# The experts' second layer as seven block products in place of eight

## The chip, the cores and the metric

The kernel runs on one core of a Trainium2 chip. The metric is the device time of one execution in microseconds, median of the runs shown. The kernel issues work to TensorE (PE for its matmuls, PEld for its weight loads), VectorE (DVE), ScalarE (ACT), GpSimd (POOL) and the DMA queues of SyncE (SP).

## The reference

One layer of a graph network over 6,250 tokens of width 256, in float32. A graph attention part and a mixing part are added to `x`; then every token passes through a mixture of experts. All tokens share one routing decision, so the same 2 of 8 experts serve all of them. Only this last part is touched:

```
xf = layernorm(x)                                        # 6250 x 256
h = gelu(einsum('nd,edf->enf', xf, W1) + b1)             # per expert 6250 x 512
y = einsum('enf,efd->end', h, W2) + b2                   # per expert 6250 x 256
out = x + layernorm(sum over 2 experts of w_e * y_e + xf) * gamma + beta
```

## The kernel before

The tokens are cut into 25 blocks (`NB`) of 250 (`BT`), each of two token tiles (`TB`) of 125 (`TP`); in an output row a token has its own partition, 125 in all. Up to about 465 us of the profile the kernel makes the graph part, the mixing part, the residual and the normalised rows, which stay in SBUF. Then the routing picks two experts, their weights are loaded (`load_expert`, SP and ACT queues), and VectorE multiplies the second layer's weights `w2s` by the routing weights `tw` in place (L1803) and makes the offset row `b2w` (L1804, L1806). From there on only the experts run.

TensorE goes by a pipeline written out in program order: `hidden(b)`, then `result(b-1)`, for b from 1 to 25 (in the last step `result` alone). `hidden(b)` (L1231) makes eight tiles of 128 hidden features (`NF` = 4 for each of two experts) by 250 tokens, each over two halves of the width, in PSUM banks 0 to 3. ScalarE turns each tile to `ge` with gelu and the bias (L951), double buffered over blocks. `result(b)` (L1244) makes, for each of the two token tiles, one PSUM tile of 125 tokens by 256 outputs as a sum of eight matmuls, four for each expert; `ge` is the stationary operand (125 columns), `w2s` the moving one (256 columns). Its banks are 4 to 7, two for a block, so that two blocks are in flight.

A float32 matmul stands in the profile as two passes, each with its own weight load: 400 matmuls of `result` are "x800".

VectorE finishes a tile of 125 tokens n = 0 to 49: `make_z` adds the PSUM tile to the row `za` (L1826), takes the moments (L1828, L1830); `make_row` prepares the next `za` (L1815, L1818); `make_y` centres and scales by gamma (L1837) and, with the inverse deviation from POOL, makes the output row (L1844). POOL makes that deviation in `z_scale` (L663, L665) and adds beta to the residual row in `x_and_offset` (L671), in this order by tile. SP stores a block's output when its second tile is done (L494; for the last block each tile alone, L497).

Every wait is a semaphore wait written out in the instruction stream of its engine, and each engine works in program order. `idle_work` (L977) is a filler, matmuls of `ones` by `ident`, 128 moving columns, which keep TensorE going in gaps of the middle part; it has no part in the result.

Of the kernel before, what the change touches and what calls it, by code (L numbers as in the profile page):

```python
# [11 lines left out]
ALU = mybir.AluOpType  # L12
# [10 lines left out]
TOP_K = 2  # L23
CAPACITY_FACTOR = 1.25
TP = 125
TB = 2
# [31 lines left out]
def gps_layer(nc, x, idx_dst, idx_src, w_gnn, attn_l, attn_r, w_qkv, bn_gamma, bn_beta, w_dw, w_pw,  # L58
# [43 lines left out]
    with ExitStack() as ctx:  # L102
# [102 lines left out]
        skr = take(NH * BT)  # L205
        sqr = take(NH * BT)
        US = 3
        u = take(US * TB * D).rearrange("p (a t d) -> p a t d", a=US, t=TB)
        nsb = take(BT)
        vk = take(NH * BT)  # L210
# [16 lines left out]
        take = cut((0, LW, L))  # L227
        za = take(2 * D).rearrange("p (a d) -> p a d", a=2)

        def zc(b, c0, n=1):  # L230
            return Z[:, b * ZW + c0 * BT:b * ZW + (c0 + n) * BT]
# [125 lines left out]

        f_done = stage("f_done", TOP_K * NF)
        gelu_done = stage("gelu_done", TOP_K * NF)
        y_done = stage("y_done", TB)  # L360

        z_row = stage("z_row", 2)
        z = stage("z", 3)
        z_rstd = stage("z_rstd", 2)
        z_gam = stage("z_gam", 1)
        x_bet = stage("x_bet", 1)
# [55 lines left out]
        def res_bank(b, t):  # L422

            if b < NB - 1:
                return ps[0:TP, 6, t * D:(t + 1) * D]
            return ps[0:TP, (R_K, R_Q)[t], 0:D]

        def uses(b, ring):

# [74 lines left out]
        def _(pool):  # L504
# [161 lines left out]

            def x_and_offset(n):

                pool.wait_ge(z_row.sem, z_row.count(n, 1))
                at_ = x_of(n // TB, n % TB)  # L670
                g.tensor_tensor(at_, at_, bet[0:TP, :], ALU.add).then_inc(x_bet.sem, 1)  # L671

            pool.wait_ge(ln_in, 32)
            x_and_offset(0)
            for n in range(TB * NB):
                z_scale(n)
                if n + 1 < TB * NB:
                    x_and_offset(n + 1)

        @block.scalar  # L680
        def _(act):
# [262 lines left out]
            def gelu(b):  # L944
                for f in range(TOP_K * NF):
                    if b == 0 and f % NF == 0:
                        act.wait_ge(b1_in[f // NF], 16)
                    act.wait_ge(f_done.sem, f_done.count(b, f + 1))
                    if f == 0 and b >= 2:
                        act.wait_ge(y_done.sem, y_done.count(b - 2))  # L950
# [6 lines left out]
        def _(pe):  # L957
# [275 lines left out]
                    last.then_inc(f_done.sem, 1)  # L1233

            def result(b):
                for t in range(TB):
                    if b == 0 and t == 0:
                        pe.wait_ge(w_dve, 5)
                    if b >= 2:
                        pe.wait_ge(z.sem, z.count(TB * (b - 2) + t, 1))  # L1240
                    for f in range(TOP_K * NF):
                        if t == 0:
                            pe.wait_ge(gelu_done.sem, gelu_done.count(b, f + 1))
                        last = mm(ps[0:TP, 4 + 2 * (b % 2) + t, 0:D], ge[:, b % 2, f, t * TP:(t + 1) * TP],  # L1244
                                  w2s[:, f // NF, f % NF, :], start=(f == 0), stop=(f == TOP_K * NF - 1))
                    last.then_inc(y_done.sem, 1)
# [4 lines left out]
            pipeline(1, NB + 1, [(0, lambda b: hidden(b) if b < NB else None), (0, lambda b: result(b - 1))])  # L1251

        @block.vector
        def _(dve):
# [545 lines left out]
            for i in range(TOP_K):  # L1800
                dve.wait_ge(w2_in[i], 32)
                wi = w2s[:, i].rearrange("p f d -> p (f d)")
                v_.tensor_scalar(wi, wi, tw[:, i:i + 1], None, ALU.mult).then_inc(w_dve, 1)  # L1803
            v_.tensor_scalar(b2w[0:TP], b2s[0:TP, 0], tw[0:TP, 0:1], None, ALU.mult).then_inc(w_dve, 1)  # L1804
# [5 lines left out]
            def make_row(n):  # L1810

                b, t = n // TB, n % TB
                if n >= 2:
                    dve.wait_ge(z.sem, z.count(n - 2, 1))
                v_.tensor_scalar(za[0:TP, n % 2], x_of(b, t), mv2[0:TP, b, t, 0:1], rstd2[0:TP, b, t:t + 1],  # L1815
                                 ALU.subtract, ALU.mult).then_inc(z_row.sem, 1)
                dve.wait_ge(z_row.sem, z_row.count(n, 1))
                v_.tensor_tensor(za[0:TP, n % 2], za[0:TP, n % 2], b2w[0:TP], ALU.add).then_inc(z_row.sem, 1)  # L1818

            def make_z(n):  # L1820
                b, t, a = n // TB, n % TB, n % 2
                dve.wait_ge(z_row.sem, z_row.count(n))
                dve.wait_ge(y_done.sem, y_done.count(b, t + 1))
                if n >= 2:
                    dve.wait_ge(z_gam.sem, z_gam.count(n - 2))
                v_.tensor_tensor(zz[0:TP, a], ps[0:TP, 4 + 2 * (b % 2) + t, 0:D], za[0:TP, a], ALU.add).then_inc(z.sem, 1)  # L1826
                wait_apart(dve, z, z.count(n, 1))
                v_.bn_stats(zst[0:TP, a], zz[0:TP, a]).then_inc(z.sem, 1)  # L1828
                wait_apart(dve, z, z.count(n, 2))
                v_.bn_aggr(zmv[0:TP, a], zst[0:TP, a]).then_inc(z.sem, 1)  # L1830

            def make_y(n):
                b, t, a = n // TB, n % TB, n % 2
# [3 lines left out]
                v_.scalar_tensor_tensor(out=zg[0:TP, a], in0=zz[0:TP, a], scalar=zmv[0:TP, a, 0:1], in1=gam[0:TP],  # L1837
                                        op0=ALU.subtract, op1=ALU.mult).then_inc(z_gam.sem, 1)
                if t == 0 and b >= 2:
# [4 lines left out]
                v_.scalar_tensor_tensor(out=yo[0:TP, b % 2, t], in0=zg[0:TP, a], scalar=zr[0:TP, a, 1], in1=x_of(b, t),  # L1844
                                        op0=ALU.mult, op1=ALU.add).then_inc(y_ready.sem, 1)
# [55 lines left out]
```

## Time and profile before

| | |
|---|---|
| time, median of 3 runs | 822.78 us (822.64, 822.78, 825.34) |
| span of the profiled execution | 820.6 us |
| median time less that span | 2.2 us |
| the experts' part | from 471.9 us to the end |
| mean granted TensorE clock | 0.984 |
| TensorE matmul / weight load busy | 95% / 78% |
| VectorE / ScalarE / GpSimd busy | 63% / 52% / 47% |

The profiled execution's own time is not reported beside its span; the span runs from the first to the last instruction, and what lies around it is taken as the 2.2 us between the span and the median. Busy time of TensorE is the time in which at least one matmul is in flight, and matmuls are pipelined, so the spacing of matmuls says more than the share. "x32" at a row of the timeline is the number of passes that were merged into it, its duration reaching from the first one's start to the last one's end. A few matmul records can be missing.

### The profile page before, as it was taken

To read this page: it belongs to the slowest core of one execution; us is meant where nothing else is said; L and a number is where in the kernel's file an instruction comes from. 1 tells how busy PE (TensorE), PEld (TensorE's weight loads), DVE (VectorE), ACT (ScalarE), POOL (GpSimd) and SP (SyncE) were. 2 spreads that over 40 slices of the span, in tenths; PEclk is the share of its full clock that TensorE was granted. 3 is DMA by queue.
4 is the path that set the end of the run, shared out by engine and by line. 5 is a ranking of instruction groups with operands and counts; after the bars stand their busy time and mean duration, and the time that the engine had idled before them with its cause. 6 is when DMAs were issued, how large, how long until landed. Compare 5 with 4: busy or idle time off the path is not lost. (4 is left out here: it accounts for less than half of the span.)

```text
span 820.6 us, 15099 instructions
## 1 busy us (share of the span) xinstructions
PE 780.2 (95%) x5056; PEld 642.5 (78%) x5056; DVE 519.0 (63%) x1475; ACT 426.2 (52%) x969; POOL 383.1 (47%) x601
## 2 busy tenths in 40 slices
PE   5899999999899999999489999999999999999996
PEld 4778888888566676666256888888888888888885
DVE  6863488797779888888988534343434343444445
ACT  2566336898999898888376143232323232323230
POOL 3430888777458888888457402222222222222222
PEclk9999999999999999999889899999999999999999
DMA  8855122222012121111101130000000000000000
GB/s 213 203 161 151 42 59 51 56 54 53 16 51 66 33 66 32 53 56 40 42 24 30 37 99 21 19 21 18 21 17 21 18 21 17 22 17 22 17 22 29
DMA packets 35420, 41.31 MB, mean 50 GB/s; under 512 B 11520, under 2 KB 20696, under 8 KB 35339
## 3 DMA queue, kind: packets, MB, share of 16 engines
q1 hardware_dynamic: 22355, 30.71, 13.0%
q0 software_dynamic: 8000, 6.82, 3.8%
q10 hardware_dynamic: 4984, 2.79, 1.4%
q8 instruction: 40, 0.66, 0.3%
q14 instruction: 41, 0.34, 0.1%
HBM read 25.59 MB, written 14.60 MB: 49 GB/s over the span
## 5 line engine op out<-in xcount | busy, mean ns | idle before, releaser
L951 ACT ACTIVATE Z<-ps,b1s 128x250 f32<-128x250 f32 x200 | 93.5, 469 | 233.1 <-PE ps L1231 233.1
L1244 PE MATMUL ps<-Z 128*125 128x256 f32 x800 | 176.6, 380 | 0.0
L1231 PE MATMUL ps<-Z 128*128 128x250 f32 x800 | 173.2, 374 | 0.0
L1244 PEld LDWEIGHTS ps<-Z 128*125 128x125 f32 x800 | 150.2, 188 | 22.2
L1231 PEld LDWEIGHTS ps<-Z 128*128 128x128 f32 x800 | 151.7, 190 | 17.4
L663 POOL TENSOR_SCALAR zr<-zmv 125x1 f32<-125x1 f32 x50 | 11.1, 221 | 249.0 <-issue 240.1
L1025 PE MATMUL ps<-Z,L 128*128 128x250 f32 x600 | 126.9, 374 | 0.0
L1025 PEld LDWEIGHTS ps<-Z,L 128*128 128x128 f32 x600 | 113.9, 190 | 12.9
L1826 DVE TENSOR_TENSOR Z<-ps,L 125x256 f32<-125x256 f32 x50 | 21.2, 425 | 161.0 <-PE ps L1244 161.0
L1145 PE MATMUL ps<-wr,Z 128*125 128x256 f32 x400 | 92.7, 385 | 0.0
L790 ACT ACTIVATE Z<-Z,bn_o,bn_s 128x250 f32<-128x250 f32 x150 | 81.2, 598 | 1.0 <-DVE bn_o L1535 1.0
L1145 PEld LDWEIGHTS ps<-wr,Z 128*125 128x125 f32 x400 | 73.1, 188 | 10.2 <-issue 0.4
L1035 PE MATMUL ps<-Z,pw 64*64 64x250 f32 x600 | 54.6, 386 | 17.0 <-issue 15.3
L1416 DVE BATCH_NORM_STATS2 L<-Z 128x6 f32<-128x250 f32 x140 | 49.2, 408 | 26.4 <-ACT Z L786 24.2
L532 POOL DMA_INDIRECT L<-xt_table,idst x36 | 44.5, 1236 | 38.7 <-issue 37.6
L786 ACT ACTIVATE Z<-ps 128x500 f32<-128x500 f32 x75 | 43.4, 579 | 30.9 <-PE ps L1025 25.1
L1035 PEld LDWEIGHTS ps<-Z,pw 64*64 64x64 f32 x600 | 25.9, 134 | 38.0 <-issue 25.4
L535 POOL DMA_INDIRECT asrc<-xt_table,isrc x40 | 48.7, 1217 | 12.2 <-issue 12.2
L1004 PE MATMUL ps<-L,Z 128*125 128x264 f32 x200 | 51.8, 405 | 0.0
L1123 PE MATMUL ps<-L,ones 128*32 128x250 f32 x600 | 47.4, 377 | 1.5 <-issue 0.8
L1844 DVE SCALAR_TENSOR_TENSOR Z<-Z,zr 125x256 f32<-125x256 f32 x50 | 41.1, 822 | 9.5 <-POOL zr L665 6.2
L671 POOL TENSOR_TENSOR Z<-Z 125x256 f32<-125x256 f32 x50 | 36.1, 722 | 20.8 <-DVE L L1815 20.8
(221 smaller groups left out, 1274.7 us busy)
## 6 DMA issues: line engine op xcount, KB each, us to landing
Z<-in_x SPq DMA_DIRECT2D x25, 250.0 KB
out<-Z SPq DMA_DIRECT2D x24, 250.0 KB
xt_table<-L SPq DMA_DIRECT2D x25, 231.0 KB
Z<-in_x SPq DMA_DIRECT2D x1, 2016.0 KB
g_table<-gt SPq DMA_DIRECT2D x25, 62.5 KB
gr<-g_table SPq DMA_DIRECT2D x25, 62.5 KB
Z<-in_x SPq DMA_DIRECT2D x1, 1344.0 KB
Z<-in_w SPq DMA_DIRECT2D x2, 512.0 KB, 3.4
```

The costliest lines, as they stand in the source:

```text
L532: g.indirect_dma_start(rows_at[:, t, :], None, xt_table, bass.IndirectOffsetOnAxis(ap=idst[0:TP, j:j + 1].bitcast(U32), axis=0)).then_inc( ...
L535: g.indirect_dma_start(left_at[:, t, :], None, xt_table, bass.IndirectOffsetOnAxis(ap=isrc[0:TP, j:j + 1].bitcast(U32), axis=0), element_o ...
L790: a_.activation(zc(b, c), zc(b, c), ACT.Relu, bias=bn_o[:, c:c + 1], scale=bn_s[:, c:c + 1]).then_inc(done.sem, 1)
L951: a_.activation(ge[:, b % 2, f, :], ps[:, f % 4, 0:BT], ACT.Gelu, bias=b1s[:, f // NF, f % NF:f % NF + 1]).then_inc(gelu_done.sem, 1)
L1004: last = mm(ps[0:TP, 2 + 2 * (b % 2) + t, 0:XT], h_raw(b, k)[:, t * TP:(t + 1) * TP], wg[:, k, :], start=(k == 0), stop=(k == KD - 1))
L1025: last = mm(ps[:, group_bank(n), h * BT:(h + 1) * BT], wq[:, k, c * 128:(c + 1) * 128], h_raw(b, k), start=(k == 0), stop=(k == KD - 1))
L1035: return mm(to[cols_], lhsT[rows_, HALF * a:HALF * a + HALF], rhs[rows_], start=True, stop=True)
L1123: last = mm(ps[32 * q:32 * q + 32, 5, 0:BT], ones[:, 0:32], of, start=(i == 0), stop=(i == 3), skip_group_check=True)
L1145: last = mm(res_bank(b, t), ob(b, c, 1)[:, t * TP:(t + 1) * TP], wr[:, c, :], start=(c == 0), stop=(c == NO - 1))
L1231: last = mm(ps[:, f % 4, 0:BT], w1s[:, f // NF, k, (f % NF) * 128:(f % NF + 1) * 128], h_of(b, k), start=(k == 0), stop=(k == KD - 1))
L1244: last = mm(ps[0:TP, 4 + 2 * (b % 2) + t, 0:D], ge[:, b % 2, f, t * TP:(t + 1) * TP], w2s[:, f // NF, f % NF, :], start=(f == 0), stop=(f ...
L1416: v_.bn_stats(to, ps[:, group_bank(n), h * BT:(h + 1) * BT] if last else zc(b, c)).then_inc(z_sums.sem, 1)
```

## The change

For a block, write the hidden features of expert e and token tile t as A[e,t], and the weights of expert e and output half l (128 outputs) as W[e,l]. Before, each of four results Y[t,l] is the sum over the two experts of A[e,t] W[e,l]: eight block products, done as four pairs of width 256. After, they come from seven products (Strassen's scheme in the form with few sums), each of four matmuls (k = 0 to 3) with 125 stationary and 128 moving columns:

- POOL makes four sums of `ge` tiles for each block (`sums_of_g`, 125 x 500 of each, into `gs`, double buffered). It does so for block b+1 ahead of `z_scale` of block b.
- VectorE makes four sums of weight tiles once (`wt`, 128 x 512 each), between the scaling of `w2s` and the row `b2w`.
- TensorE issues the products in the order P1, P5, P6, P3, P7, P2, P4 into three banks (X, Z, Y = 4, 5, 6). P6, P7 and P4 accumulate onto bank X, P3 onto bank Z. Since each partial sum is read on the way, a product that reuses a bank waits for VectorE's read of it: P6 for that of P1, P3 for that of P5, P7 for that of P6, P4 for that of P7. One product lies between in each case. P1 of a block waits for all seven reads of the block before.
- VectorE reads each product with one `tensor_tensor` of 125 x 128 from PSUM (`take_parts`, seven for a block in place of two of 125 x 256), and the rest of a block's rows is regrouped: moments of both tiles, the next block's rows, centring, their offset, both outputs.
- The last block's `result` keeps the old form (`last_result`), with banks X and Y and a wait on all reads of the block before.

The diff, cut:

```diff
+            def sums_of_g(b):
+                a, n = b % 2, g_sums
+                pool.wait_ge(gelu_done.sem, gelu_done.count(b))
+                if b >= 2:
+                    pool.wait_ge(y_part.sem, y_part.count(b - 2))
+                g.tensor_tensor(gs[:, a, 0], ge_part(b, 0, 1), ge_part(b, 1, 1), ALU.add).then_inc(n.sem, 1)
+                pool.wait_ge(n.sem, n.count(b, 1))
+                g.tensor_tensor(gs[:, a, 1], gs[:, a, 0], ge_part(b, 0, 0), ALU.subtract).then_inc(n.sem, 1)
+                pool.wait_ge(n.sem, n.count(b, 2))
+                g.tensor_tensor(gs[:, a, 3], ge_part(b, 1, 0), gs[:, a, 1], ALU.subtract).then_inc(n.sem, 1)
+                g.tensor_tensor(gs[:, a, 2], ge_part(b, 0, 0), ge_part(b, 0, 1), ALU.subtract).then_inc(n.sem, 1)
             pool.wait_ge(ln_in, 32)
-            x_and_offset(0)
-            for n in range(TB * NB):
-                z_scale(n)
-                if n + 1 < TB * NB:
-                    x_and_offset(n + 1)
+            sums_of_g(0)
+            for t in range(TB):
+                x_and_offset(t)
+            for b in range(NB):
+                if b + 1 < NB - 1:
+                    sums_of_g(b + 1)
+                for t in range(TB):
+                    z_scale(TB * b + t)
+                if b + 1 < NB:
+                    for t in range(TB):
+                        x_and_offset(TB * (b + 1) + t)
...
+                for n in (P1, P5, P6, P3, P7, P2, P4):
+                    if n == P1:
+                        if b == 0:
+                            pe.wait_ge(w_dve, 3)
+                        else:
+                            pe.wait_ge(y_sum.sem, y_sum.count(b - 1))
+                        pe.wait_ge(gelu_done.sem, gelu_done.count(b))
+                    if n == P5:
+                        if b == 0:
+                            pe.wait_ge(w_sums, 4)
+                        pe.wait_ge(g_sums.sem, g_sums.count(b))
+                    if n == P6:
+                        pe.wait_ge(y_sum.sem, y_sum.count(b, KEPT_1))
+                    if n == P3:
+                        pe.wait_ge(y_sum.sem, y_sum.count(b, KEPT_5))
+                    if n == P7:
+                        pe.wait_ge(y_sum.sem, y_sum.count(b, KEPT_U))
+                    if n == P4:
+                        pe.wait_ge(y_sum.sem, y_sum.count(b, SUM_22))
+                    for k in range(NF):
+                        last = mm(ps[0:TP, bank[n], 0:HD2], of[n][:, k], by[n][:, k], start=(n in first and k == 0),
+                                  stop=(k == NF - 1), skip_group_check=True)
+                    last.then_inc(y_part.sem, 1)
+            def last_result(b):
+                for t in range(TB):
+                    if t == 0:
+                        pe.wait_ge(y_sum.sem, y_sum.count(b - 1))
...
+            v_.tensor_tensor(wt(1), half(0, 1), half(0, 0), ALU.subtract).then_inc(w_sums, 1)
+            v_.tensor_tensor(wt(3), half(1, 1), half(0, 1), ALU.subtract).then_inc(w_sums, 1)
+            dve.wait_ge(w_sums, 1)
+            v_.tensor_tensor(wt(2), half(1, 1), wt(1), ALU.subtract).then_inc(w_sums, 1)
+            dve.wait_ge(w_sums, 3)
+            v_.tensor_tensor(wt(4), half(1, 0), wt(2), ALU.subtract).then_inc(w_sums, 1)
...
+                for after, to, part, other, needs in (
+                        (P1, kz[0:TP, 0], x_, za[0:TP, 0, lo], None),
+                        (P5, kz[0:TP, 1], z_, za[0:TP, 1, hi], None),
+                        (P6, kz[0:TP, 2], x_, za[0:TP, 0, hi], None),
+                        (P3, zz[0:TP, 0, hi], z_, kz[0:TP, 2], KEPT_U),
+                        (P7, zz[0:TP, 1, hi], x_, kz[0:TP, 1], KEPT_5),
+                        (P2, zz[0:TP, 0, lo], y_, kz[0:TP, 0], KEPT_1),
+                        (P4, zz[0:TP, 1, lo], x_, za[0:TP, 1, lo], None)):
+                    dve.wait_ge(y_part.sem, y_part.count(b, after))
+                    if needs:
+                        dve.wait_ge(y_sum.sem, y_sum.count(b, needs))
+                    v_.tensor_tensor(to, part, other, ALU.add).then_inc(y_sum.sem, 1)
...
-            make_row(0)
-            for n in range(TB * NB):
-                make_z(n)
-                if n + 1 < TB * NB:
-                    make_row(n + 1)
-                make_y(n)
+            make_rows(0)
+            offset_rows(0)
+            for b in range(NB - 1):
+                take_parts(b)
+                dve.wait_ge(y_sum.sem, y_sum.count(b))
+                for t in range(TB):
+                    moments(b, t)
+                make_rows(b + 1)
+                for t in range(TB):
+                    center(TB * b + t)
+                offset_rows(b + 1)
+                for t in range(TB):
+                    make_y(TB * b + t)
```

## Rows read from the trace of the kernel before

**Rows 1.** The page: busy time and share of each engine.
```profile
PE 780.2 (95%) x5056; PEld 642.5 (78%) x5056; DVE 519.0 (63%) x1475; ACT 426.2 (52%) x969; POOL 383.1 (47%) x601
```

**Rows 2.** Busy time by stretch: us, then busy us (records) of each engine, clock, DMA.
```profile
600.00:700.00 100.00, 100.00 (x470) 88.34 (x470) 45.12 (x108) 26.98 (x58) 24.41 (x47) 1.00 0.06 19
```

**Rows 3.** The waits from 470 us on: engine, line, releaser, us, times, longest.
```profile
DVE Z L1826 <- PE ps L1244: 161.0, 24, 6.7
```

**Rows 4.** Timeline of one block: start us, us, engine, line, operation, merged count.
```profile
561.18 6.92 PE L1231 MATMUL ps<-Z 128*128 128x250 f32 x32
...
567.94 7.07 PE L1244 MATMUL ps<-Z 128*125 128x256 f32 x32
...
571.65 0.42 DVE L1826 TENSOR_TENSOR Z<-ps,L 125x256 f32<-125x256 f32 x1 [6.73 <-PE ps L1244]
...
574.85 2.49 PE L1231 MATMUL ps<-Z 128*128 128x250 f32 x11
```

**Rows 5.** Timeline: weight loads of fillers, and of matmuls with one moving column.
```profile
454.99 0.97 PEld L977 LDWEIGHTS ps<-ident,ones 128*128 128x128 f32 x8
...
461.83 0.97 PEld L1201 LDWEIGHTS ps<-ones,L 125*128 125x128 f32 x8
```

**Rows 6.** The filler's own line, all of its passes: ns minimum, median, maximum.
```profile
L977 PEld LDWEIGHTS ps<-ident,ones x118: 186/192/339, 16.2 to 471.7; 128*128 128x128 f32 x118
L977 PE MATMUL ps<-ident,ones x118: 275/276/582, 16.6 to 471.8; 128*128 128x128 f32 x118
```

**Rows 7.** Timeline: VectorE's end releases TensorE.
```profile
464.48 0.16 DVE L1751 TENSOR_TENSOR rtot<-rtot,ps 128x2 f32<-128x2 f32 x1 [1.05 <-PE ps L1201]
...
464.69 0.13 PEld L1206 LDWEIGHTS ps<-rt_w,rtot 128*1 128x1 f32 x4 [0.41 <-DVE rtot L1751]
```

**Rows 8.** Single lines, ns minimum, median, maximum: VectorE and POOL operations by inputs.
```profile
L1581 DVE TENSOR_TENSOR Z<-ps,L x25: 668/670/680, 213.5 to 442.9; 128x500 f32<-128x500 f32 x25
...
L1663 DVE SCALAR_TENSOR_TENSOR L<-ps,se,brow x50: 474/480/485, 227.7 to 455.2; 125x256 f32<-125x256 f32 x50
...
L1844 DVE SCALAR_TENSOR_TENSOR Z<-Z,zr x50: 485/877/883, 492.3 to 817.0; 125x256 f32<-125x256 f32 x50
```

**Rows 9.** Groups by form: a small POOL operation of the same kind.
```profile
L599 POOL TENSOR_TENSOR cc<-cc 125x2 f32<-125x2 f32 x25 | 4.8, 194 | 2.1
```

**Rows 10.** Timeline: POOL beside VectorE, twice in the experts' part, once before.
```profile
300.09 1.43 POOL L606 TENSOR_TENSOR Z<-Z,gr 125x256 f32<-125x256 f32 x2
...
300.95 0.88 DVE L1663 SCALAR_TENSOR_TENSOR L<-ps,se,brow 125x256 f32<-125x256 f32 x2
...
563.92 0.72 POOL L671 TENSOR_TENSOR Z<-Z 125x256 f32<-125x256 f32 x1
564.04 0.88 DVE L1844 SCALAR_TENSOR_TENSOR Z<-Z,zr 125x256 f32<-125x256 f32 x1
```

**Rows 11.** Timeline and landing: start of the experts' part.
```profile
475.89 0.42 SPq L490 DMA_DIRECT2D Z<-in_beta  x1
...
DMA to landing us min/median/max: 5.0/5.0/5.0
...
480.33 1.42 DVE L1803 TENSOR_SCALAR Z<-Z,tw 128x1024 f32<-128x1024 f32 x2 [0.92 <-DMA Z<-in_b]
...
485.94 7.07 PE L1244 MATMUL ps<-Z 128*125 128x256 f32 x32
```

**Rows 12.** Busy time by stretch around the last fall of the clock.
```profile
463.00:464.00 1.00, 0.81 (x7) 0.81 (x8) 0.40 (x3) 0.00 (x0) 0.00 (x0) 0.98 0.00 0
...
470.00:471.00 1.00, 1.00 (x7) 1.00 (x7) 0.00 (x0) 0.00 (x0) 0.00 (x0) 0.60 1.04 403
```

**Rows 13.** Timeline of the end.
```profile
800.29 13.98 PE L1244 MATMUL ps<-Z 128*125 128x256 f32 x64
...
814.36 0.42 DVE L1826 TENSOR_TENSOR Z<-ps,L 125x256 f32<-125x256 f32 x1
...
817.03 0.48 DVE L1844 SCALAR_TENSOR_TENSOR Z<-Z,zr 125x256 f32<-125x256 f32 x1 [0.82 <-POOL zr L665]
```

More of the change, by code:

```diff
@@ L207, in gps_layer @@
         US = 3
+        U0 = 2 * NC * BT + NC * BT + NO * BT + 2 * NH * BT
+        U1 = U0 + US * TB * D
         u = take(US * TB * D).rearrange("p (a t d) -> p a t d", a=US, t=TB)
@@ L226, in gps_layer @@
         yo = take(2 * TB * D).rearrange("p (a t d) -> p a t d", a=2, t=TB)
-        take = cut((0, LW, L))
-        za = take(2 * D).rearrange("p (a d) -> p a d", a=2)
+        take = cut((0, U0, L))
+        za = take(TB * D).rearrange("p (a d) -> p a d", a=TB)
+        gs = take(2 * 4 * NF * TP).rearrange("p (a i f n) -> p a i f n", a=2, i=4, f=NF)
+        kz = take(3 * 128).rearrange("p (i d) -> p i d", i=3)
+        take = cut((U1, LW, L))
+        wt0 = take(3 * NF * 128).rearrange("p (i f d) -> p i f d", i=3, f=NF)
+        take = cut((U0 - NF * 128, U0, L))
+        wt3 = take(NF * 128).rearrange("p (f d) -> p f d", f=NF)
         def zc(b, c0, n=1):
@@ L359, in gps_layer @@
         gelu_done = stage("gelu_done", TOP_K * NF)
-        y_done = stage("y_done", TB)
+        y_done = sem("y_done")
         z_row = stage("z_row", 2)
-        z = stage("z", 3)
+        z = stage("z", 2)
+        y_sum = stage("y_sum", 7)
+        y_part = stage("y_part", 7)
+        g_sums = stage("g_sums", 4)
+        w_sums = sem("w_sums")
         z_rstd = stage("z_rstd", 2)
@@ L426, in res_bank, with ge_part, wt @@
             return ps[0:TP, (R_K, R_Q)[t], 0:D]
+        X_BANK, Z_BANK, Y_BANK = 4, 5, 6
+        P1, P5, P6, P3, P7, P2, P4 = range(1, 8)
+        KEPT_1, KEPT_5, KEPT_U, SUM_12, SUM_22, SUM_11, SUM_21 = range(1, 8)
+        HD2 = D // 2
+        assert TB == 2 and TOP_K == 2 and HD2 == 128
+        def ge_part(b, e, t):
+            return ge[:, b % 2, NF * e:NF * e + NF, t * TP:(t + 1) * TP]
+        def wt(i):
+            return wt3 if i == 4 else wt0[:, i - 1]
         def uses(b, ring):
@@ L1250, in _ @@
             weights_of_two()
-            pipeline(1, NB + 1, [(0, lambda b: hidden(b) if b < NB else None), (0, lambda b: result(b - 1))])
+            pipeline(1, NB + 1, [(0, lambda b: hidden(b) if b < NB else None), (0, lambda b: result(b - 1) if b < NB else last_result(NB - 1))])
         @block.vector
@@ L1832, in make_y, with make_rows, offset_rows @@
-            def make_y(n):
-                b, t, a = n // TB, n % TB, n % 2
+            def make_rows(b):
+                if b:
+                    dve.wait_ge(y_sum.sem, y_sum.count(b - 1))
+                for t in range(TB):
+                    v_.tensor_scalar(za[0:TP, t], x_of(b, t), mv2[0:TP, b, t, 0:1], rstd2[0:TP, b, t:t + 1],
+                                     ALU.subtract, ALU.mult).then_inc(z_row.sem, 1)
+            def offset_rows(b):
+                for t in range(TB):
+                    dve.wait_ge(z_row.sem, 4 * b + 1 + t)
+                    v_.tensor_tensor(za[0:TP, t], za[0:TP, t], b2w[0:TP], ALU.add).then_inc(z_row.sem, 1)
@@ new lines, in _, with take_parts @@
+            lo, hi = slice(0, HD2), slice(HD2, D)
+            def take_parts(b):
+                dve.wait_ge(z_row.sem, 4 * b + 4)
+                x_, z_, y_ = (ps[0:TP, bank, 0:HD2] for bank in (X_BANK, Z_BANK, Y_BANK))
+                if b:
+                    dve.wait_ge(z_gam.sem, z_gam.count(TB * b - 1))
+                for after, to, part, other, needs in (
[10 more added lines that the diff above has]
+                    v_.tensor_tensor(to, part, other, ALU.add).then_inc(y_sum.sem, 1)
@@ L1834, in make_y, with moments, center @@
+            def moments(b, t):
+                n = TB * b + t
+                v_.bn_stats(zst[0:TP, t], zz[0:TP, t]).then_inc(z.sem, 1)
+                wait_apart(dve, z, z.count(n, 1))
+                v_.bn_aggr(zmv[0:TP, t], zst[0:TP, t]).then_inc(z.sem, 1)
+            def center(n):
+                t = n % TB
                 dve.wait_ge(z.sem, z.count(n))
```

57 lines of the change are left out of this document (29 added, 28 removed).

## The prediction

> **What bounds the kernel now.** I read the page first: TensorE is busy for 780 of 820.6 us and no other engine for more than 519 [rows 1]. An average says little about one stage, so I went to the busy time by stretch. The change touches only the part behind 471.9 us; between 600 and 700 us TensorE is busy for all of the 100 us, VectorE for 45, POOL for 24 [rows 2]. The waits agree: VectorE's longest total is 161 us spent on the result matmuls [rows 3]. The timeline then gives the unit. Hidden matmuls start at 561.18, results at 567.94, the next hidden ones at 574.85 [rows 4]: a block is 13.67 us, 6.76 for `hidden` and 6.91 for `result`, with no gap. 64 result passes in a row take 13.98 us [rows 13]; with 0.38 for the last, a pass starts every 13.60 / 63 = 0.216 us. So 32 x 0.216 = 6.91 us for a block's result, and whatever is saved there is saved in full as long as TensorE keeps its feed.
>
> **Removed and added on TensorE.** In 24 blocks 32 passes of 256 columns become 7 products x 4 matmuls x 2 passes = 56 passes of 128. By columns alone a pass would take 0.108 us (half of 0.216), 6.05 us for a block. But halving the columns leaves each weight load as large as before, and the load needs to fit in the shadow of the pass ahead. Passes of 128 columns with full loads stand in the trace as fillers: eight loads in 0.97 us at 0.192 each [rows 5, 6], so (0.97 - 0.19) / 7 = 0.111 us from one to the next. Loads for matmuls of one moving column come at the same spacing, (0.97 - 0.19) / 7 [rows 5]. So a load has a pace of about 0.11 us of its own and a pass of 128 columns the same: they just balance, side by side. I take 0.111: 56 x 0.111 = 6.22 us, 0.69 less than 6.91, and **24 x 0.69 = 16.6 us gained**. Bounds: 0.108 gives 20.6 us; 0.113, had a filler pass lost 2 ns more than its rows show by rounding, gives 13.9. Break even is at 6.91 / 56 = 0.123 us.
>
> The Trainium skill ("TensorE: Matmul & The Clock Gate", section "Back-to-back issue gap") speaks against the change: in a stream of load and matmul pairs of 128 columns it has about 81 ns a pair where the columns alone give 56, since both operations set the spacing. An estimate from that page's ratio, 1.45 x 0.108 = 0.156 us, would make a result 8.8 us and cost 45 us in all; the fillers at 0.111 don't agree with it.
>
> **The new loop between TensorE and VectorE.** Four products of a block wait until VectorE has read a product, and one product, 8 x 0.111 = 0.89 us, lies between. Let s be the start of a product's last pass. The pass ends at s + 0.28 [rows 6]. VectorE follows the modelled end by 0.09: the 16th result pass began at 567.94 + 15 x 0.216 = 571.18, ended 0.38 later, and VectorE began at 571.65 [rows 4]. Its read of 256 columns takes 0.42 and a like one of 500 takes 0.67 [rows 4, 8], about 1.0 ns a column, so one of 128 takes 0.29. TensorE answers 0.05 after VectorE's end (464.64 to 464.69) [rows 7]. Sum: s + 0.71. The waiting product's first load is wanted one pass ahead of its turn, at s + 0.89. Spare: about 0.18 us. I cost the four waits at nothing; the cover is the product between, and if it is gone each wait costs its lateness, 24 x 4 times.
>
> The seven reads must not be slowed by POOL, which makes its sums just then. Two SBUF inputs on VectorE do suffer: L1844 takes 0.485 alone and 0.877 in the median, and at 564.04 it ends 0.28 after POOL's L671 has ended [rows 8, 10], as if its 256 elements went only after POOL's operation. An operation with one input in PSUM doesn't: two of L1663 at 300.95 lie mostly inside POOL's 300.09 to 301.52 and all fifty take 474 to 485 ns [rows 8, 10]. The new reads are of this second kind.
>
> **VectorE between blocks.** Last read of a block to first of the next: 6.76 for `hidden` and 0.89 for P1. The work there is the old one regrouped: 45.12 us busy in 100 [rows 2] are 6.17 in a block of 13.67, less two reads of 0.42 [rows 4] 5.3, waits for POOL's beta additions included. With gaps of 0.1 between some six dependent ones it takes 5.9 us, and 7.3 are there. Hidden.
>
> **POOL.** L671 takes 0.72 for 256 elements [rows 10] and an operation of two takes 0.19 [rows 9], so 2.1 ns an element and 1.22 us for 500. Four sums with gaps of 0.1 take 5.2; what it did before is 24.41 us in 100 [rows 2], 3.3 a block; with locks that is under 10 of a block's 12.98 us. The sums of b+1 start when gelu of b+1 is done, beside result(b), and are wanted after hidden(b+2), 7 us after they end. z_scale stands behind them in POOL's order, but its moments come only after result(b). Hidden. ScalarE's new waits are on things done a block earlier; nothing.
>
> **The first block** is where the sums are late. Before, VectorE had w2 scaled at 481.75 and results began at 485.94 [rows 11]. Now POOL starts its four sums when beta has landed, 475.89 + 5.0 = 480.9 [rows 11]; VectorE's second scaling and its four weight sums (512 elements, 0.69 each by the 500's 0.67 [rows 8]) fall into them. If the lock goes operation by operation, each of POOL's runs about 1.1 after the other's end and each of VectorE's about 0.5: 4 x 1.15 + 5 x 0.5 + gaps = 7.4, so the weight sums are done at 488.4. Behind them stand six operations of 256 columns (two for b2w, two rows, two offsets), 0.4 each like L1826 [rows 4], and two waits of 0.6 for POOL's beta additions, since the offsets have two SBUF inputs: 3.6 in all, the first read at 492.0, its end at 492.3. P1 ends at 486.8, P5 runs 488.4 to 489.3, P6 and the other four from 492.4 to 496.9; without waits it would be 485.94 + 6.22 = 492.1. **Lost: 4.8 us.** Bounds: 0.3 if no lock shows, 5.5 if POOL's elements are slower than L671's.
>
> With TensorE idle for 1.6 and 3 us there, the clock may fall. Its last fall, from 2.4 to 1.2 GHz, came just before 464 us (0.98 in that us), when the stream had thinned, and it came back during 470 to 471 (0.60 is full speed in the last fifth), 6.8 us later [rows 12]. [...] Bounds 0 and 3.4 (half of those 6.8 us).
>
> **The last block.** Its result waits for all reads: with s as above for the last product of block 23, it starts at s + 0.71 and a load of 0.19 later. Its 16th pass starts at s + 0.9 + 15 x 0.216 = 4.1, and the first tile is ready 0.47 later, at 4.6. But VectorE has the 5.9 us of regrouped work behind its last read (s + 0.66 to 6.6) and takes it only at 6.6. A tile's chain from read to output is 817.51 - 814.36 = 3.15 us [rows 13], two one behind the other end at 12.9. In the old form the last pass starts at s + 32 x 0.216 = 6.9, and the end is 0.47 + 3.15 later, at 10.5. **Lost: 2.4 us.**
>
> **Sum** against the span: 820.6 - 16.6 + 4.8 + 2.2 + 2.4 = 813.4; with the 2.2 us between span and median, 815.6 us, 0.9% faster. What a measurement can tell from no change is 0.5%, 4.1 us.
>
> **The rivals.**
> - *The start is milder* (no clock fall, or little lock). For it: the clock fell only after thin work for a few us. It gives 804.8 (all low bounds) to 813.4. Chance 0.13; the forecast itself 0.55.
> - *The loop is late by a little.* If a read of 128 columns costs as much as one of 256 (0.42) and the answer takes 0.15, the sum is 0.94, late by 0.05; with slips at each product 0.06 x 4 x 24 = 5.8 us, 821.4: no change. For it: the spare is small. Against: durations follow the columns. 0.14.
> - *Slower: POOL's sums hold up the reads of PSUM.* A read then waits half a POOL operation, 0.56: the loop is 1.27, late by 0.39, 37 us in 24 blocks, 853. It decides from a lateness of 0.17 (4 x 0.17 = 0.69). Against: all fifty L1663. 0.09.
> - *Loads no longer hide*, since the fillers load the same `ones` each time and `ge` tiles differ: load and pass one after the other, 0.11 + 0.11 = 0.22 a pass, 12.3 for a result, 5.4 x 24 = 130 us, 953; anything above 0.123 is a loss. Against: the loads of L1201 differ too and keep 0.111 [rows 5]. 0.04. (The Trainium skill's section named above is a milder form of it.)
> - *POOL becomes the bound*, if its sums over strided tiles take 2.5 us instead of 1.22: 15.0 for a block against 12.98, 24 x 2.0 = 48 us, 864. Break even needs 2.1. Against: same operation and type as L671. 0.05.
>
> Faster by over 0.5%: 0.55 + 0.13 = 0.68. Within: 0.14. Slower: 0.09 + 0.04 + 0.05 = 0.18. The forecast's own terms reach from 806 to 820; taking in the little lateness, 806 to 823 holds 8 in 10.
>
> **What would show it.** In the changed profile: 56 result passes a block at 0.111 us (a block of 12.98), TensorE without idle at P6, P3, P7, P4; reads of 0.29 us; POOL's sums of 1.22 us ending before the block's reads do; VectorE's two-input operations near 482 to 491 us stretched, results of block 0 ending near 497, the clock perhaps at 0.5 there; an end some 5 us behind the last matmul. It would be wrong if a pass takes over 0.12, or if idle stands before each waiting product.

## The result, and the profile after

The changed kernel takes 810.03 us in the median of four runs (807.92 to 812.95) against 822.78 for the kernel before (822.64 to 825.34, four runs): ratio 0.984, 95% interval 0.981 to 0.987. The forecast was 815.6 with 806 to 823. The profiled execution is the fastest of the four; its span is 806.1 us, 14.5 less than before.

The page's first part and one stretch of the busy time by stretch answer to [rows 1, 2]. (Columns: engine, busy us, share, instructions; for the stretch: busy us of PE, PEld, DVE, ACT, POOL with records, granted clock, DMA share, GB/s.)

```profile
PE 762.1 (95%) x5632; PEld 643.2 (80%) x5632; DVE 549.7 (68%) x1599; ACT 426.4 (53%) x969; POOL 509.6 (63%) x697
```

```profile
600.00:700.00 100.00, 100.00 (x686) 94.52 (x685) 54.26 (x147) 29.54 (x63) 66.73 (x79) 1.00 0.07 22
```

TensorE is still without a gap, with more and shorter passes; POOL's work has nearly tripled and VectorE's has grown by a fifth, and neither shows in the time. One block in the timeline, to be set beside [rows 4] (start us, us, engine, line, operation, merged count, idle before and its releaser):

```profile
604.99 1.03 PE L1310 MATMUL ps<-Z 128*125 128x128 f32 x8
...
605.86 1.91 PE L1310 MATMUL ps<-L 128*125 128x128 f32 x16
606.16 0.29 DVE L1927 TENSOR_TENSOR L<-ps,L 125x128 f32<-125x128 f32 x1 [2.20 <-PE ps L1310]
...
607.07 1.15 POOL L708 TENSOR_TENSOR L<-L,Z 128x500 f32<-128x500 f32 x1
...
611.10 6.93 PE L1278 MATMUL ps<-Z 128*128 128x250 f32 x32
...
617.86 1.04 PE L1310 MATMUL ps<-Z 128*125 128x128 f32 x8
```

A block is 617.86 - 604.99 = 12.87 us (13.67 before), and its result 611.10 - 604.99 = 6.11 us (6.91 before). 6.11 / 56 is 0.1091 us a pass. From the first product of block 1 (501.96 us) to that of block 23 (785.25) every block takes 12.88 us, so 24 x (13.67 - 12.88) = 19.0 us are gained in the blocks with seven products. The single lines of the reads and of POOL's first sum (ns minimum, median, maximum):

```profile
L1927 DVE TENSOR_TENSOR Z<-ps,L x96: 291/292/293, 492.8 to 791.6; 125x128 f32<-125x128 f32 x96
L1927 DVE TENSOR_TENSOR L<-ps,L x72: 280/292/293, 490.4 to 788.1; 125x128 f32<-125x128 f32 x72
```

```profile
L706 POOL TENSOR_TENSOR L<-Z x24: 1246/1250/1277, 480.9 to 773.1; 128x500 f32<-128x500 f32 x24
```

No read of a product is longer than 0.293 us, though POOL's sums run beside them. What was given back lies at the two ends. The start, to be set beside [rows 11]:

```profile
480.37 2.41 DVE L1880 TENSOR_SCALAR Z<-Z,tw 128x1024 f32<-128x1024 f32 x2 [0.58 <-DMA Z<-in_b]
...
482.30 1.49 POOL L708 TENSOR_TENSOR L<-L,Z 128x500 f32<-128x500 f32 x1
482.81 1.53 DVE L1883 TENSOR_TENSOR L<-Z 128x512 f32<-128x512 f32 x1
...
486.31 1.03 PE L1310 MATMUL ps<-Z 128*125 128x128 f32 x8
...
488.18 1.14 PE L1310 MATMUL ps<-L 128*125 128x128 f32 x8 [0.83 <-DVE L L1888]
...
489.60 0.76 DVE L1906 TENSOR_TENSOR L<-L,Z 125x256 f32<-125x256 f32 x2
490.38 0.49 DVE L1927 TENSOR_TENSOR L<-ps,L 125x128 f32<-125x128 f32 x2
...
490.73 1.14 PE L1310 MATMUL ps<-L 128*125 128x128 f32 x8 [1.41 <-DVE L L1927]
...
495.20 6.93 PE L1278 MATMUL ps<-Z 128*128 128x250 f32 x32
```

VectorE's weight sum takes 1.53 us beside POOL's sum of 1.49, P5 starts at 488.18 and P6 at 490.73; block 0's result takes 495.20 - 486.31 = 8.89 us, 2.78 more than 6.11. The granted clock stays at 1.00 (2.4 GHz) in this execution. The end, to be set beside [rows 13]:

```profile
790.49 1.04 PE L1310 MATMUL ps<-L,Z 128*125 128x128 f32 x8
...
791.91 7.17 PE L1321 MATMUL ps<-Z 128*125 128x256 f32 x32 [0.39 <-DVE Z L1927]
...
797.03 0.41 DVE L1972 TENSOR_TENSOR Z<-ps,L 125x256 f32<-125x256 f32 x1
...
802.62 0.48 DVE L1950 SCALAR_TENSOR_TENSOR Z<-Z,zr 125x256 f32<-125x256 f32 x1 [0.82 <-POOL zr L691]
```

The last pass of block 23 starts at 790.49 + 7 x 0.109 = 791.25, and VectorE ends at 803.10, 11.85 later. In the profile before it is 10.5: block 23's last pass starts at 800.29 + 31 x 0.216 = 806.99, VectorE ends at 817.51 [rows 13]. That is 1.35 us lost. The first pass of all results comes 0.37 later than before (486.31 for 485.94 [rows 11]), from the part ahead, which the change does not touch. Together: -19.0 + 2.8 + 1.35 + 0.4 = -14.5, the whole difference of the spans.

### The profile page after: what moved, and what is told of

Its sections match the earlier page's. It is cut to its first block and busy times, and to the rows that moved or that the text cites. A ratio compares the mean times of both kernels' runs of the same rounds, so it can differ in the third digit from the quotient of the medians.

```text
span 806.1 us, 16493 instructions
## 1 busy us (share of the span) xinstructions
PE 762.1 (95%) x5632; PEld 643.2 (80%) x5632; DVE 549.7 (68%) x1599; ACT 426.4 (53%) x969; POOL 509.6 (63%) x697
## 5 line engine op out<-in xcount | busy, mean ns | idle before, releaser
L1278 PEld LDWEIGHTS ps<-Z 128*128 128x128 f32 x800 | 149.6, 189 | 17.4 <-DMA Z<-in_w 1.0
L1310 PE MATMUL ps<-L 128*125 128x128 f32 x576 | 71.1, 273 | 2.2 <-DVE L L1927 1.4
L1927 DVE TENSOR_TENSOR L<-ps,L 125x128 f32<-125x128 f32 x72 | 20.9, 292 | 75.4 <-PE ps L1310 75.4
L706 POOL TENSOR_TENSOR L<-Z 128x500 f32<-128x500 f32 x24 | 30.0, 1252 | 62.8 <-ACT Z L998 44.6
L1310 PEld LDWEIGHTS ps<-L 128*125 128x125 f32 x576 | 66.7, 188 | 2.6 <-DVE L L1927 1.6
L1927 DVE TENSOR_TENSOR Z<-ps,L 125x128 f32<-125x128 f32 x96 | 28.0, 292 | 55.8 <-PE ps L1310 55.8
L561 POOL DMA_INDIRECT asrc<-xt_table,isrc x40 | 48.4, 1210 | 12.2 <-issue 12.2
L698 POOL TENSOR_TENSOR Z<-Z 125x256 f32<-125x256 f32 x50 | 53.7, 1092 | 2.6 <-DVE L L1900 2.6
L689 POOL TENSOR_SCALAR zr<-zmv 125x1 f32<-125x1 f32 x50 | 13.1, 262 | 58.7 <-issue 47.7
```

Of the source, the lines that this page charges most:

```text
L561: g.indirect_dma_start(left_at[:, t, :], None, xt_table, bass.IndirectOffsetOnAxis(ap=isrc[0:TP, j:j + 1].bitcast(U32), axis=0), element_o ...
L1278: last = mm(ps[:, f % 4, 0:BT], w1s[:, f // NF, k, (f % NF) * 128:(f % NF + 1) * 128], h_of(b, k), start=(k == 0), stop=(k == KD - 1))
L1310: last = mm(ps[0:TP, bank[n], 0:HD2], of[n][:, k], by[n][:, k], start=(n in first and k == 0), stop=(k == NF - 1), skip_group_check=True)
L1927: v_.tensor_tensor(to, part, other, ALU.add).then_inc(y_sum.sem, 1)
```

## The experiments

Each median stands beside that of the kernel before, run together with it on the same chip. These medians of the kernel before differ by up to 1.4 us between sets (822.78 in the section above), so two versions are compared directly only where this column agrees, and otherwise by their distance from it.

| run | median us | before, same chip | ratio, interval |
|---|---|---|---|
| changed kernel again | 810.95 | 824.21 | 0.983 (0.981 to 0.985) |
| result in halves | 825.36 | 824.21 | 1.002 (1.000 to 1.003) |
| block 0 plain | 806.98 | 824.21 | 0.979 (0.977 to 0.981) |
| first and last block | 806.06 | 824.21 | 0.977 (0.975 to 0.980) |
| P4 uncovered | 828.33 | 823.49 | 1.006 (1.004 to 1.008) |
| late reads | 813.82 | 823.49 | 0.989 (0.985 to 0.993) |
| more sums (one run) | 816.24 | 823.49 | |
| bank 7 | 812.70 | 823.49 | 0.986 (0.983 to 0.989) |
| changed kernel, third | 810.47 | 823.07 | 0.984 (0.982 to 0.986) |
| fillers | 810.42 | 823.07 | 0.985 (0.983 to 0.988) |

**The changed kernel again.** No edit.

> The changed kernel once more, unaltered, with more runs, to see its spread. So far four runs gave 807.9, 808.2, 811.9 and 813.0 us. Theory A: the spread comes from the idle stretch of TensorE in the first block (487.3 to 490.7 us in the profile), after which the clock falls in some executions: the same two levels about 4 us apart should show, and the higher ones should have a lower mean clock. Rival B: the spread comes from the part ahead of the experts, where the clock falls once in every execution, and the first block has no part in it.

All five runs lie between 810.35 and 813.75 us. The profiled one, the slowest of them, shows what the first profile didn't: behind the idle stretch the clock is at half.

```profile
489.63 1.04 PE L1310 MATMUL ps<-Z 128*125 128x128 f32 x8
...
492.71 1.81 DVE L1906 TENSOR_TENSOR L<-L,Z 125x256 f32<-125x256 f32 x2
...
494.89 1.70 PE L1310 MATMUL ps<-L 128*125 128x128 f32 x8 [2.46 <-DVE L L1927]
...
501.03 5.24 PE L1278 MATMUL ps<-Z 128*128 128x250 f32 x24
```

```profile
494.00:495.00 1.00, 0.10 (x1) 0.11 (x2) 0.97 (x3) 0.00 (x0) 1.00 (x2) 1.00 0.00 0
...
496.00:497.00 1.00, 1.00 (x6) 1.00 (x6) 0.29 (x1) 0.00 (x0) 0.92 (x2) 0.50 0.00 0
...
499.00:500.00 1.00, 1.00 (x12) 1.00 (x11) 0.29 (x1) 0.00 (x0) 0.11 (x1) 1.00 0.00 0
```

From P6 to the next hidden layer 6.14 us go by (501.03 - 494.89) where the first profile has 4.47: 1.67 us of clock. And P6 itself comes 0.8 later, since the two offset rows took 1.81 us in place of 0.76: VectorE and POOL's beta addition took their turns in the other order. So the same program loses 2.8 or 5.3 us here. But the spread is not settled by it. Two levels 4 us apart didn't show in these five runs, and the slower ones have no lower mean clock (0.984 and 0.981 for the two slowest, 0.986, 0.984 and 0.982 for the others), so theory A failed. The kernel before spreads over 822.50 to 826.79 beside them, with no such idle stretch. The traces show a second place: the first product starts at 489.63 us here, at 486.31 in the first profile, though the program is the same. Of the 5.8 us between the two spans 3.3 arise ahead of the first product and 2.5 in block 0. That is rival B's place; why the part ahead varies was not looked into.

**Halving the columns alone.** The kernel before, with

```diff
-                    for f in range(TOP_K * NF):
+                    for l in range(2):
+                        cols = slice(l * 128, (l + 1) * 128)
+                        for f in range(TOP_K * NF):
...
-                        last = mm(ps[0:TP, 4 + 2 * (b % 2) + t, 0:D], ge[:, b % 2, f, t * TP:(t + 1) * TP],
-                                  w2s[:, f // NF, f % NF, :], start=(f == 0), stop=(f == TOP_K * NF - 1))
+                            last = mm(ps[0:TP, 4 + 2 * (b % 2) + t, cols], ge[:, b % 2, f, t * TP:(t + 1) * TP],
+                                      w2s[:, f // NF, f % NF, cols], start=(f == 0), stop=(f == TOP_K * NF - 1),
```

> The kernel before, with each result of 256 moving columns cut into two of 128, nothing else: 64 passes of 128 columns for 32 of 256 in each of 25 blocks, with twice the weight loads. Theory: loads of 125 columns hide behind passes of 128 and a pass costs 0.109 us as in the changed kernel's profile, 64 x 0.109 = 6.98 us for 6.91 in a block, 25 x 0.07 = 1.7 us slower in all. Rival: loads don't quite hide and the pace of the changed kernel has another cause: with 0.12 us a pass it is 19 us slower, with 0.156 some 77 us slower.

```profile
486.91 7.15 PE L1246 MATMUL ps<-Z 128*125 128x128 f32 x64
...
493.90 6.29 PE L1231 MATMUL ps<-Z 128*128 128x250 f32 x29
```

6.99 us for 64 passes, 0.109 each, and 1.2 us more in the median (2.0 by the traces' 0.08 a block; 1.7 expected). With twice the loads and unlike stationary tiles the load still hides. This settles the rival of loads that don't hide.

**Block 0 in the old form.** VectorE's four weight sums go behind the rows, and POOL's sums begin with block 1.

```diff
-            sums_of_g(0)
...
-(0, lambda b: result(b - 1) if b < NB else last_result(NB - 1))
+(0, lambda b: plain_result(b - 1) if b - 1 in (0, NB - 1) else result(b - 1))
```

> The changed kernel with block 0 in the old form (32 passes of 256 columns), so that VectorE makes the sums of the weights while TensorE works on block 0, and POOL makes no sums for it. Theory: block 0's result costs 6.91 us instead of the 8.89 from 486.31 to 495.20 us in the profile of the changed kernel, 2.0 us faster in span, 804.1 us; and since TensorE no longer stands idle there (theory A of the first run), no run lies 4 us above the others, so that the median gains 2 to 5 us. Rival B: the span gains 2.0 us and the spread stays.

```profile
484.75 0.68 DVE L1963 TENSOR_TENSOR L<-Z 128x512 f32<-128x512 f32 x1
...
486.32 7.07 PE L1334 MATMUL ps<-Z 128*125 128x256 f32 x32
...
493.23 6.92 PE L1292 MATMUL ps<-Z 128*128 128x250 f32 x32
```

With POOL's sums out of the way a weight sum takes 0.68 us, against 1.53 to 1.65. Block 0 takes 6.91 us, the span is 804.1 as expected, and the median falls by 4.0 us against the unaltered kernel run beside it. The spread (805.9 to 809.1) is as wide as before, so it has its source elsewhere. By these medians block 0's result takes 6.91 + 4.0 = 10.9 us in the changed kernel; against 6.11 it loses 4.8. Each of the two medians is known to some 1.7 us (from the intervals above), so the 4.8 is rough. The three profiles of the unaltered kernel have 8.9, 11.4 and 13.0 us, a loss of 2.8, 5.3 and 6.9.

**First and last block.** On top of it, the last block's first tile goes to bank 7, and VectorE interlocks its two tiles:

```diff
+                moments(b, t)
+                if t:
+                    make_y(TB * b)
+                center(TB * b + t)
+            make_y(TB * b + 1)
```

> As the run before, and the last block's first tile goes to the free bank 7, so that TensorE starts it without waiting for VectorE's last reads, while VectorE takes the second tile's sum before it finishes the first one's output. Theory: the last block loses 1.35 us in the changed kernel, since VectorE is still busy with block 23 and then handles two tiles one behind the other; with the tiles interlocked the end moves to 3.05 us behind TensorE's end, which itself is 0.6 us earlier: 1.0 to 1.5 us faster than the run before, a span of 802.8 us. Rival: VectorE's work of block 23 sets the start of the first tile and the gain is under 0.5 us.

```profile
789.26 1.04 PE L1321 MATMUL ps<-L,Z 128*125 128x128 f32 x8
...
790.14 7.07 PE L1334 MATMUL ps<-Z 128*125 128x256 f32 x32
...
797.43 0.42 DVE L1991 TENSOR_TENSOR Z<-ps,L 125x256 f32<-125x256 f32 x1
...
800.05 0.49 DVE L1955 SCALAR_TENSOR_TENSOR Z<-Z,zr 125x256 f32<-125x256 f32 x1 [0.52 <-DVE Z L1945]
```

From block 23's last product to VectorE's end 11.28 us go by where the changed kernel has 12.61: 1.3 us, as expected, and 0.9 in the median. The expected span of 802.8 us did not come in the profiled execution, which has 804.2: its first result pass starts at 487.07 for 486.32 in the run before, and 3.7 us follow VectorE's end where that run has 3.0. A gain of 0.9 between medians of five runs that spread over 3 us is not clear of noise; what shows the gain is the trace. This version has the lowest median, 806.06 us, 18 below the kernel before and 5 below the changed one.

**A wait without cover.** P4 directly behind P7.

```diff
-                for n in (P1, P5, P6, P3, P7, P2, P4):
+                for n in (P1, P5, P6, P3, P7, P4, P2):
```

> The changed kernel with P4 issued directly behind P7, whose read by VectorE it waits for, and P2 last: one of the four waits loses the product that covers it. It measures the loop from TensorE over VectorE and back. Theory: the loop from the start of a product's last pass to the next first load is 0.27 + 0.03 + 0.29 + 0.05 = 0.65 to 0.71 us, and without cover TensorE loses that, less 0.11 and plus a load that nothing hides (0.1 to 0.2): 0.65 to 0.8 us in each of 24 blocks, 16 to 19 us slower. Rival: the waits are satisfied otherwise than I read (the loop is longer, 1 us or more, hidden by the queue): over 24 us slower; or shorter, under 10.

```profile
607.71 0.29 DVE L1927 TENSOR_TENSOR Z<-ps,L 125x128 f32<-125x128 f32 x1 [0.58 <-PE ps L1310]
...
608.05 1.14 PE L1310 MATMUL ps<-L,Z 128*125 128x128 f32 x8 [0.38 <-DVE Z L1927]
...
609.90 6.93 PE L1278 MATMUL ps<-Z 128*128 128x250 f32 x32
...
623.42 3.76 PE L1278 MATMUL ps<-Z 128*128 128x250 f32 x17
```

A block is 13.52 us, 0.65 more. TensorE answers 0.05 us after the read's end (608.00). P7's last pass starts at 607.40, 0.31 ahead of the read, so the loop is 0.31 + 0.29 + 0.05 = 0.65 us; less the 0.11 until the next pass would have started and plus 0.10 for a load that nothing hides it is the 0.65 lost (rounded). The one cover taken away costs 24 x 0.65 = 15.6 us, more than the 13 us that the change gains in all. By the medians it is 17.4 to 18.1 us; what the other 2 are was not found, and the spread of such a set is as large.

**A longer loop.**

```diff
+                    v_.tensor_tensor(jz[0:TP, after - 1], part, za[0:TP, 0, lo], ALU.add).then_inc(jz_done, 1)
                     v_.tensor_tensor(to, part, other, ALU.add).then_inc(y_sum.sem, 1)
```

> The changed kernel with each of the seven reads of a product preceded by one more operation of the same form (125 x 128 from PSUM, into a tile that nobody uses), which makes the loop 0.29 us longer. The spare of the loop is read as 0.17 us. Theory: every one of the four waits becomes 0.12 us late, 0.5 us a block, 11 to 13 us slower in all, the break even with the kernel before. Rival: the spare is larger than 0.29 (VectorE's second read of a tile starts nearer to the end of the product): no change, within 2 us. If the spare were nil: 28 us slower.

```profile
609.69 1.98 PE L1312 MATMUL ps<-L 128*125 128x128 f32 x16
609.99 0.29 DVE L1929 TENSOR_TENSOR xg<-ps,L 125x128 f32<-125x128 f32 x1 [2.00 <-PE ps L1312]
610.20 0.28 DVE L1930 TENSOR_TENSOR L<-ps,L 125x128 f32<-125x128 f32 x1
```

The expectation of 11 to 13 us missed, and so did its rival of no change: a block is 12.95 us, only 0.07 more, all of it in the joined P5 and P6 (1.98 for 1.91). The miss is in what the edit added: of two operations with no wait between, the second starts 0.21 after the first, not 0.29. With that the sums fit: P1 is read from 0.41 behind its last pass's start, the others from 0.31. 0.41 + 0.21 + 0.28 + 0.05 = 0.95 is 0.07 to 0.08 past the 8 x 0.109 = 0.87 at which the next load is wanted, and 0.85 for the others is inside. The spare of the unaltered loop is 0.12 us at P6 and 0.22 at the other three. Against the kernel before the median is 2.9 to 3.6 us above the changed kernel's; the blocks account for 24 x 0.07 = 1.7 of it, the rest is within the spread of these four runs (812.25 to 817.64).

**Twice the sums on POOL.**

```diff
+                for i in range(4):
+                    if i >= 2:
+                        pool.wait_ge(jg_done, 4 * b + i - 1)
+                    g.tensor_tensor(jg[:, i % 2], ge_part(b, 0, 0), ge_part(b, 0, 1), ALU.subtract).then_inc(jg_done, 1)
```

> The changed kernel with four more sums of the same form on POOL in every block (from the same tiles, into tiles that nobody uses), ahead of the last real sum. Theory: POOL's work grows from 8.6 us in a block of 12.87 (66.7 us busy in 100) by 4 x 1.16 + gaps to 13.3 or 13.5 us, POOL becomes the bound and the kernel is 10 to 16 us slower, with VectorE's waits for POOL in the profile. VectorE's reads from PSUM keep their 0.292 us though POOL's sums now run beside all of them. Rival: POOL's sums hold up VectorE's reads as well: reads above 0.3 us and over 30 us slower.

POOL's groups between 600 and 700 us (line, operation, count, busy us, mean ns, idle before):

```profile
L716 POOL TENSOR_TENSOR xg<-Z 128x500 f32<-128x500 f32 x32 | 33.4, 1077 | 0.0
L700 POOL TENSOR_TENSOR Z<-Z 125x256 f32<-125x256 f32 x15 | 12.0, 818 | 0.0
L708 POOL TENSOR_TENSOR L<-Z 128x500 f32<-128x500 f32 x8 | 10.0, 1250 | 2.7 <-ACT Z L1004 2.7
```

The expectation was wrong: a block stays at 12.88 us. POOL is busy for 94.9 of these 100 us, 12.2 in a block, and just fits. I had taken 4 x 1.16 for the new sums, which take 4.2 together, and had added them to a busy time that held waits: the beta addition, 1.10 in the mean in the changed kernel, takes 0.82 here, twice a block. 8.6 + 4.2 - 0.6 = 12.2. This single run is 5.4 to 6.0 us slower against the kernel before than the changed kernel. Block 0 bears part of that: its P5 waits 6.0 us for POOL's last sum, and its result takes 503.53 - 487.92 = 15.6 us where the unaltered profiles have 8.9 to 13.0. The reads keep 0.29 us.

**Bank 7 alone.** The last block's first tile in bank 7, VectorE as it was.

```diff
-                    if t == 0:
+                    if t:
                         pe.wait_ge(y_sum.sem, y_sum.count(b - 1))
```

> The changed kernel with the last block's first tile in the free bank 7, so that TensorE needn't wait for the last reads of block 23; VectorE's order is unchanged. Theory: TensorE starts 0.6 us earlier, but VectorE is busy with block 23 until 797.1 us and takes the first tile no earlier, so the end doesn't move: within 0.2 us in span. Rival: TensorE's wait sets the end and it comes 0.6 us earlier.

```profile
796.93 1.04 PE L1310 MATMUL ps<-L,Z 128*125 128x128 f32 x8
...
797.80 7.07 PE L1321 MATMUL ps<-Z 128*125 128x256 f32 x32
...
809.05 0.48 DVE L1950 SCALAR_TENSOR_TENSOR Z<-Z,zr 125x256 f32<-125x256 f32 x1 [0.82 <-POOL zr L691]
```

TensorE starts 0.87 behind P4's start in place of 1.42, and VectorE ends 809.53 - 796.93 = 12.60 behind it, as before (12.61). The end is VectorE's. The spans can't show it: this one is 812.6 us, since its first product starts at 490.04 and its block 0 takes 11.6 us. The median, 10.8 us below the kernel before where the unaltered kernel is 12.6 to 13.3 below, shows no gain either.

**Idle time or clock.**

> The changed kernel unaltered, as the measure for the run beside it, on the same chip. In the profiled executions of it and of its relatives so far the first block's result took 8.9 us with the clock at full speed throughout (one of them), and 11.4 to 11.8 us where the clock fell to half behind the idle stretch (four). I expect the second.

```diff
                         if b == 0:
+                            idle_work(7, 3)
                             pe.wait_ge(w_sums, 4)
...
                     if n == P6:
+                        if b == 0:
+                            idle_work(7, 9)
                         pe.wait_ge(y_sum.sem, y_sum.count(b, KEPT_1))
```

> The changed kernel with twelve filler matmuls (128 x 128 by 128 columns, into the free bank 7) in the first block, three in front of the wait of P5 and nine in front of the wait of P6, in time that TensorE otherwise idles. They tell the idle time from the fall of the clock. Theory: of the 5.3 us that the first block loses when the clock falls, 1.6 us are work at half speed; with fillers the clock stays up, the block's result takes 9.0 to 9.8 us in the profile, and the median is 1.5 to 2 us below the unaltered kernel's. Rival: the fall of the clock costs nothing by itself, since TensorE waits for VectorE at that time anyway: the same median within 0.5 us, or above it where the fillers come late.

The control, then the fillers (PE records of both; for the control also the us in which the clock fell, the columns as in the busy time by stretch above):

```profile
493.01 2.07 PE L1310 MATMUL ps<-L 128*125 128x128 f32 x8 [2.46 <-DVE L L1927]
...
500.44 5.87 PE L1278 MATMUL ps<-Z 128*128 128x250 f32 x27
```

```profile
492.00:493.00 1.00, 0.00 (x0) 0.00 (x0) 0.97 (x3) 0.00 (x0) 1.00 (x2) 0.65 0.00 0
```

```profile
489.46 2.17 PE L1024 MATMUL ps<-ident,ones 128*128 128x128 f32 x18
...
492.10 1.14 PE L1313 MATMUL ps<-L 128*125 128x128 f32 x8 [0.47 <-DVE L L1930]
...
496.56 6.93 PE L1278 MATMUL ps<-Z 128*128 128x250 f32 x32
```

In the profiles it went by the theory: the control's clock is at half from 492.3 to 499.1 us and P6 to hidden takes 7.43 us, 2.96 more than the 4.47 at full clock; with fillers it takes 4.46 at full clock. The sizes were off: the control's result takes 13.0 us for the 11.4 to 11.8 expected, the filler run's 9.9. The medians, 810.47 and 810.42 us, don't differ, so the expected gain of 1.5 to 2 us did not come, and by the time alone it went by the rival. One execution each can't say whether the timed ones kept the clock; what the clock costs in the median stays open. The wait for VectorE is the same in both, P6 3.9 and 3.8 us late.

## Why the prediction was right, and where its sizes were off

The direction, the mechanism of the gain and the places of both losses held; the time came out 5.6 us below the point and inside the range. Three costed terms were off, all on the pessimistic side: the pass by 2.4 us, the first block by 2.2, the last by 1.05. A gain of 0.9% was forecast and 1.6% came. The time also lies within what the rival of a milder start gave (804.8 to 813.4), and the first profile, with no fall of the clock and 2.8 us lost, is that rival; the other two profiles of the same kernel, with the fall, are not.

- **The pass.** 0.111 us was taken, 0.1091 measured: 19.0 us gained for 16.6. The lower bound by columns alone (0.108) was nearer. The fillers load 128 stationary columns and the products 125, with 128 moving columns in both. In the filler run both stand in block 0 at full clock: 18 filler passes start 0.112 us apart, those of the products 0.109. The ratio is that of 128 to 125, which speaks for the load as what sets the fillers' spacing; products of 128 columns were not tried.
  The Trainium skill ("TensorE: Matmul & The Clock Gate", "Back-to-back issue gap") has both operations set the spacing at 128 columns. The size of its effect, 81 ns for 56, does not show in this float32 stream: halving the columns alone costs 0.08 us a block.
- **The loop.** Summed to 0.71 with a spare of 0.18; measured 0.65, and 0.75 at P6, with a spare of 0.22 and 0.12. At P6 it was tighter than forecast. Costed at nothing, rightly: no idle stands before P6, P3, P7 and P4 after block 0. That one product of cover is what holds it was shown by taking it away (0.65 us a block).
- **POOL beside the reads.** An operation with one PSUM input is not held up, 168 reads at 0.280 to 0.293 us; one with two SBUF inputs is, a weight sum takes 0.68 us without POOL's sums and 1.53 to 1.65 beside them. POOL's 1.22 us a sum came as 1.25, 1.16, 1.16 and 1.08.
- **The first block.** 4.8 us of waiting and 2.2 of clock were forecast, 7.0 in all. In four profiles (first, again, third, fillers) the waiting cost 2.8, 3.6, 3.9 and 3.8 us, measured from P1's start to P6's against 1.64; the clock 0, 1.7, 3.0 and 0. By the medians the whole is 4.8 us, roughly; that this is the figure forecast for the waiting alone is chance. The chain was as described (weight sums between POOL's sums, then six operations, then the read). From POOL's first sum to the end of the weight sums it took 7.2 us in all four for a forecast 7.4, from there to the first read 2.3 us in the first profile and 3.3 in the others for 3.6. The 1.0 between them are the waits for POOL's beta additions: forecast at 2 x 0.6, absent in the first profile, where the two offset rows took 0.76 us, there in the others (1.81). The 2.2 us for the clock came from no row: the rows had one stretch at half speed, 6.8 us long [rows 12], and no run shows 2.2.
- **The last block.** 1.35 us for 2.4: the regrouped work took 5.2 us, not 5.9, with hardly a gap where 0.1 was allowed for each, and each tile's chain 3.05, not 3.15. Bank 7 alone left the end where it was, so it is VectorE's work and not TensorE's wait that sets it, as the forecast had it.
- **Slips in its working,** none of which moves the point. The break even at 0.123 us a pass leaves out the 9.4 us that the same sum loses at the two ends; with them it is at (6.91 - 9.4/24) / 56 = 0.116, so the spare of the 0.111 was 5% and not 11%. The 953 us of the rival with bare loads leaves them out too (962). Half of a POOL sum of 1.22 is 0.61, not 0.56, which makes that rival some 5 us dearer. The low bounds of its own terms add to 804.8, as it says under the rivals, and not to 806.

With the measured terms, -19.0 + 4.8 + 1.35 = -12.9 us; the three sets with the unaltered kernel gave -12.8, -13.3 and -12.6. The agreement proves little, since the 4.8 was itself taken from medians. The sum that is checked is that of the two spans, -14.5, term by term from the traces.

## What to carry to other kernels

When a scheme trades multiplications for sums, ask three things of the trace: whether the smaller matmul still covers its weight load (a filler of that shape answers it), whether one piece of work lies between a read and the matmul that waits for it, and which engine pair meets where the sums are made. From such rows the length of a block could be costed to a per cent (12.98 us for 12.88), its gain, a small difference of large terms, to 13% (16.6 us for 19.0). Most of what this change gave back lay in the first block, where everything is late at once, and there the old form for one block was worth 4 us.

## What the runs showed of the hardware

- Two VectorE operations of 125 x 128 from the same PSUM tile, with no wait between, start 0.21 us apart though one lasts 0.29 (late reads).
- A stretch of 2.5 to 2.7 us in which TensorE does nothing, after another of 0.6 to 1.0 us, went with a fall to 1.2 GHz in all five profiles that had it (again, third, uncovered, late reads, bank 7); with idle stretches of 0.8 and 1.4 us (first profile) the clock stayed. The fall came 0.7 us before the matmuls began again in one and 0.4 to 1.1 us behind that in four; full clock was back 3.8 to 6.1 us after they had begun again.
- Which of VectorE and POOL goes first where each has operations with two SBUF inputs waiting differs from execution to execution of the same program: two rows' offsets took 0.76 us (first profile) or 1.81 (again, third).
- Passes of 128 moving columns start 0.112 us apart with 128 stationary columns and 0.109 with 125, in the same block at full clock (fillers).
